# Window-attention block: values computed channel-major and turned by VectorE, instead of token-major by TensorE

## The chip, the cores and the metric

The kernel runs on one core of one Trainium2 chip, in one launch. The metric is the device time of that launch in microseconds (us); the runs of the kernel before gave a median of 2942.57 us (2941.42 to 2943.20, three runs).

## The reference

The input x is [16, 192, 56, 56] in float32. The block is one layer of a shifted-window transformer; cut to what matters:

```
xl  = layernorm(x over its 192 channels) * norm1_w + norm1_b     # per pixel
xl  = roll(xl, (-3, -3));  windows of 7x7 = 49 tokens, 64 windows per image
q, k, v = xl @ qkv_w.T + qkv_b          # 6 heads of 32 channels each
attn = softmax(q @ k.T / sqrt(32))      # [49, 49] per window and head
out  = (attn @ v) @ proj_w.T + proj_b;  windows back to pixels, roll back
xl  = layernorm(out) * norm2_w + norm2_b
h   = gelu(xl @ fc1_w.T + fc1_b) @ fc2_w.T + fc2_b        # 768 hidden
return h + x
```

## The kernel before, in words

**Units and rounds.** The 56 x 56 picture is cut into 8 rows of windows. One row of windows (8 windows, T = 392 tokens) of one image is a *unit*; there are 128. The work on a unit is spread over many *rounds*: in each round every engine does one piece for several different units, in an order written out by hand in its own `step` function. `units(t)` gives the units: `u[k]` is unit t - k. The engines' own step numbers differ: round t on VectorE (DVE) and SyncE (SP) runs beside step t - 1 on GpSimd (POOL) and beside step t - 3 on TensorE (PE). Nothing but semaphores ties the engines; each runs its list strictly in order and stops at a wait.

**Precision.** Weights and activations are split into a high and a low part (`x_h`, `x_l`), and the last 64 of 192 channels hold high and low stacked in one 128-partition tile (`x_r`). So one product takes five matmuls: `five` (L317 to L324, weights stationary, 392 tokens moving, channels out) or `five_tokens` (L326 to L334, 98 tokens stationary, 192 channels moving, tokens out).

**Queries, keys, values.** `qkv` makes three tiles by `five`. `values(u, j)` (L614) makes the values token-major, one pair of windows (98 tokens) at a time: four calls in a step, twenty matmuls. `v_out` (L1061) on DVE copies each of the two PSUM banks `vt` to the tile `vs` [98 tokens, pairs, channels]. `spread` (L438) on SP then issues four DMAs from `vs` into `vbd`, in which the values of two heads stand as a block-diagonal matrix. Each takes 49 partitions, 12 runs of 128 bytes on each. `weighted` (L586) on PE reads `vbd`.

**SP's list in round t** (L451 to L468): `load_groups(t)` (xg, for the statistics of the first norm), `stats_in(t-2)` (one DMA, `bc`), `spread(t-4)`, `stats_out(t-1)` (four DMAs, waits for POOL's `rstd(0)`), `store(t-7)` (waits for DVE's `finish_main` and POOL's `residual`), and `load` (x itself, `xt`) for the unit in the slot just stored.

**POOL's list in one of its steps** (L1251 to L1275): `scaled_probs(u[4],3)`, `hidden_lo_last(u[6])`, `scaled_probs(u[3],0)`, `rstd(0,u[0])`, `less_mean_rest(u[1])`, `times_rstd_rest(u[1])`, `rstd(1,u[4])`, `scaled_probs(u[3],1)`, `residual(u[6])`, `scaled_probs(u[3],2)`. `rstd(1)` gives the reciprocal deviation of the second norm, which DVE's `normalise` (L985) waits for. `residual` (L1246) writes the last 64 output channels, which `store` waits for.

**PSUM.** Eight banks are handed round in the order of `BANK_USES` (L61); `claim` (L486) on PE waits until the last reader of the bank's previous use is done. The values' two banks are claimed as `("vt", 0)` and `("vt", 1)`; before `("vt", 1)` the bank held `("x2", 1)`, last read by DVE's `x2_rest_lo` (L991).

The functions that the change touches:

Of the kernel before, what the change touches and what calls it, by code (L numbers as in the profile page):

```python
# [22 lines left out]
F32 = mybir.dt.float32  # L23
F32R = mybir.dt.float32r
# [10 lines left out]
T = NW * N  # L35
# [53 lines left out]
QKV_READS = {4: 6, 3: 8, 2: 10}  # L89
QK_COPIES = 10  # L90

VMOVES = 16 * 4


def nth(unit, per_unit, i):

    return unit * per_unit + (i + 1)


def swin_block_program(nc, x, n1w, n1b, qkv_wt, qkv_b, proj_wt, proj_b, n2w, n2b,  # L100
                       fc1_wt, fc1_b, fc2_wt, fc2_b, out):
    ctx = ExitStack()
    with ctx:
        def sb(name, shape, dt=F32):
            return ctx.enter_context(nc.sbuf_tensor(name, shape, dt))

        def sem(name):
            return ctx.enter_context(nc.semaphore(name))
# [7 lines left out]
        wq = [sb(f"wq_{p}", [128, NQ], F32R) for p in ("mh", "ml", "rh", "rl")]  # L116
        wp = [sb(f"wp_{p}", [128, CR + C], F32R) for p in ("mh", "ml", "rh", "rl")]
        w1 = [sb(f"w1_{p}", [128, NF], F32R) for p in ("mh", "ml", "rh", "rl")]
        w2h = sb("w2h", [128, MT, C], F32R)
        w2l = sb("w2l", [128, MT, CM], F32R)  # L120
        w2r = sb("w2r", [128, MT, 128], F32R)
# [46 lines left out]
        half_k = sb("half_k", [128, 2])  # L168
        bk = sb("bk", [128, 2])

        vbd = sb("vbd", [128, 2, 2, PAIRS, 3, WP])
        vs = sb("vs", [TP, 2, PAIRS, C])
        pr = sb("pr", [TP, PAIRS, HEADS * WP])
        mx = sb("mx", [TP, PAIRS, HEADS])
        sm = sb("sm", [TP, PAIRS, HEADS])
# [20 lines left out]
        def bank(name, i):  # L196

            return psum[:, BANK_OF[name, i], :]
# [30 lines left out]
        s_hi = {n: sem(f"hi_{n}") for n in ("x1", "x2", "o")}  # L229
        s_lo = {n: sem(f"lo_{n}") for n in ("x1", "x2", "o")}  # L230
        s_qkv = sem("qkv_in_sbuf")
        s_vs = sem("values_in_sbuf")
        s_vbd = [sem(f"vbd_ready_{i}") for i in range(2)]
        s_mx = sem("row_max")
        s_sub = sem("max_subtracted")
# [55 lines left out]
        def last_read(name, i, v):  # L291

            if name in ("x2", "o"):
                return s_lo[name], v, 3, 2 * i
            if name == "ln2":
                return s_norm, v, PAIRS, 2 * i + 1
            if name == "vt":
                return s_vs, v, 2, i
            if name == "qkv":
                return s_qkv, v, QK_COPIES, QKV_READS[i] - 1  # L300
            if name == "fc1":
                return s_gelu, v, MT, i
            if name == "fc2":
                return (s_ym, s_yr)[i], v, 1, 0
            return {"s": s_sub, "pt": s_ptc}[name], v, PAIRS, i
# [69 lines left out]
        def _(sp):  # L375
# [59 lines left out]
            sp.dma_start(b2[:, 0:1], fc2_b[0:CM].rearrange("(p a) -> p a", a=1)).then_inc(s_rest, 16)  # L435
            sp.dma_start(b2[0:CR, 1:2], fc2_b[CM:C].rearrange("(p a) -> p a", a=1)).then_inc(s_rest, 16)

            def spread(u):  # L438

                sp.wait_ge(s_vs, nth(u, 2, 1))  # L440
                if u > 1:

                    sp.wait_ge(s_pe["o"], nth(u - 2, 1, 0))
                src = vs[:, u % 2].rearrange("p j (a e d) -> p (j a) e d", a=3, e=2)
                dst = vbd[:, u % 2].rearrange("p i j a d -> p i (j a) d")
                for wi in range(2):
                    for e in range(2):
                        sp.dma_start(dst[WP * e:WP * e + N, wi, :, DH * e:DH * e + DH],
                                     src[N * wi:N * wi + N, :, e, :]).then_inc(s_vbd[u % 2], 16)

            for t in range(UNITS + 7):  # L451
                if t < UNITS:
                    if t > 2:
                        load_groups(t)
                    if 1 < t < AHEAD:
                        load(0, t)
                if 0 <= t - 2 < UNITS:
                    if t - 2 > 0:
                        stats_in(t - 2)
                if 0 <= t - 4 < UNITS:  # L460
                    spread(t - 4)
                if 0 <= t - 1 < UNITS:
                    if t - 1 > 0:
                        stats_out(t - 1)
                if 0 <= t - 7 < UNITS:
                    store((t - 7) // UPB, (t - 7) % UPB)
                    if t - 7 + AHEAD < UNITS:
                        load((t - 7 + AHEAD) // UPB, (t - 7 + AHEAD) % UPB)  # L468
# [14 lines left out]
        def _(pe):  # L483
# [102 lines left out]
            def weighted(u, j):  # L586
                if j == 0:
                    pe.wait_ge(s_vbd[u % 2], nth(u // 2, VMOVES, VMOVES - 1))
                    claim(u, [("o", 0), ("o", 1)], (s_ptc, PAIRS, 0))
                else:  # L590
                    claim(u, [], (s_ptc, PAIRS, j))


                for wi, p in ((0, 0), (0, 1), (1, 0), (1, 1), (0, 2), (1, 2)):
                    if p < 2:
                        w = 2 * j + wi
                        ps = bank("o", 0)[WP * p:WP * p + WP, N * w:N * w + N]
                    else:
                        ps = bank("o", 1)[WP * wi:WP * wi + WP, N * j:N * j + N]

                    block, side = (wi, p) if p < 2 else (2, wi)
                    last = nc.tensor.matmul(ps, vbd[0:KP, u % 2, wi, j, p, :], pt[:, j, block, N * side:N * side + N],  # L602
                                            start=True, stop=True)
                if j == PAIRS - 1:
                    last.then_inc(s_pe["o"], 1)
# [5 lines left out]
                if u == 0 and tile == 4:  # L611
                    hidden_bias_products()

            def values(u, j):  # L614
                c, cc = j // 2, j % 2
                if cc == 0:
                    claim(u, [("vt", c)], (s_lo["x1"], 2, 1))
                pairs = [p[:, TP * j:TP * j + TP] for p in x1]
                last = five_tokens(bank("vt", c)[0:TP, cc * C:(cc + 1) * C], wq, pairs)
                if cc == 1:  # L620
                    last.then_inc(s_pe["vt"], 1)

            def step(t, k, it):
                u = units(t)
                if u[0] is not None:
                    values(u[0], 0)
                if u[4] is not None:
                    fc2_lo(u[4], 3)
                if u[0] is not None:
# [2 lines left out]
                    fc2_lo(u[4], 4)  # L632
                    fc2_lo(u[4], 5)
                if u[0] is not None:
                    values(u[0], 1)
                    values(u[0], 2)
                if u[3] is not None:
                    fc1(u[3], 0)
                if u[0] is not None:
                    values(u[0], 3)  # L640
                if u[3] is not None:
                    fc1(u[3], 1)
                if u[0] is not None:
# [237 lines left out]
        def _(dve):  # L881
# [9 lines left out]
            def split(n, w, raw, cols, nw, scaled):  # L891

                sm_, sr_ = raw
                dve.wait_ge(s_raw[n], 16 * (18, 6, 3)[n])
                if nw is not None:
                    if n:
                        dve.wait_ge(s_split, n)
                    nc.vector.tensor_scalar(scl_m[:, 0:cols], sm_[:, 0:cols], nwb[:, nw:nw + 1], None, ALU.mult).then_inc(s_scaled, 1)
                    nc.vector.tensor_scalar(scl_r[:, 0:cols], sr_[:, 0:cols], nwb[:, nw + 1:nw + 2], None, ALU.mult).then_inc(s_scaled, 1)
                    scaled += 2  # L900
                    dve.wait_ge(s_scaled, scaled)
                    sm_, sr_ = scl_m, scl_r
                nc.vector.tensor_copy(w[0][:, :], sm_[:, 0:cols]).then_inc(s_scaled, 1)
                nc.vector.tensor_copy(w[2][:, :], sr_[:, 0:cols]).then_inc(s_scaled, 1)
                scaled += 2
                dve.wait_ge(s_scaled, scaled)
                nc.vector.tensor_tensor(w[1][:, :], sm_[:, 0:cols], w[0][:, :].bitcast(F32), ALU.subtract)

                low = CR if n == 1 else 128
                nc.vector.tensor_tensor(w[3][0:low, :], sr_[0:low, 0:cols], w[2][0:low, :].bitcast(F32), ALU.subtract).then_inc(s_split, 1)  # L910
                return scaled
# [149 lines left out]
            def v_out(u, c):  # L1061
                if u > 1:

                    dve.wait_ge(s_vbd[u % 2], nth(u // 2 - 1, VMOVES, VMOVES - 1))
                dve.wait_ge(s_pe["vt"], nth(u, 2, c))
                nc.vector.tensor_copy(vs[:, u % 2, 2 * c:2 * c + 2, :], bank("vt", c)[0:TP, 0:2 * C].rearrange("p (j n) -> p j n", j=2)).then_inc(s_vs, 1)

            def step(t, k, it):
                u = units(t)
# [133 lines left out]
        def _(pool):  # L1203
# [26 lines left out]
            def times_rstd_rest(u):  # L1230
                pool.wait_ge(s_yr1_sub, nth(u, 1, 0))
                nc.gpsimd.tensor_tensor(yr1[:, :], yr1[:, :], bc[0:CR, u % 2, :, 1], ALU.mult).then_inc(s_yr1, 1)

            def hidden_lo_last(u):
# [2 lines left out]
                b = (MT - 1) % HB  # L1237
                nc.gpsimd.tensor_tensor(hl[:, b, :], hf[:, b, :], hh[:, b, :].bitcast(F32), ALU.subtract).then_inc(s_hl_last, 1)  # L1238

            def scaled_probs(u, j):  # L1240

                pool.wait_ge(s_rec, nth(u, PAIRS, j))
                each = rc[:, j, :].unsqueeze(2).to_broadcast([TP, HEADS, N])
                nc.gpsimd.tensor_tensor(probs(j), probs(j), each, ALU.mult).then_inc(s_prob, 1)  # L1244
# [6 lines left out]
            def step(t, k, it):  # L1251
# [10 lines left out]
                if u[1] is not None:  # L1262
                    if u[1] > 0:
                        less_mean_rest(u[1], (k - 1) % SLOTS)
                    if u[1] > 0:
                        times_rstd_rest(u[1])
                if u[4] is not None:
                    rstd(1, u[4])
                if u[3] is not None:
# [35 lines left out]
```

## Time and profile before

| | |
|---|---|
| median of three runs | 2942.57 us |
| profiled execution: span from first to last instruction | 2938.0 us |
| PE busy | 2892.5 us (98%) |
| DVE busy | 2630.3 us (90%) |
| ACT (ScalarE) busy | 2686.3 us (91%) |
| POOL busy | 1364.7 us (46%) |
| SP queue waiting for POOL's residual, in total | 947.0 us, 128 times |

The page gives no other time for the profiled execution than its span; the median of the runs is 4.6 us above it. Matmuls are pipelined, so the duration of one is longer than the distance to the next start; for what a matmul costs, starts are to be compared. An SP row in a timeline is the time that the queue needs to issue a DMA, not the transfer; "us to landing" counts from there to the last byte.

### The profile page before, as it was taken

What the parts mean: (1) busy time and instruction counts of PE and PEld (TensorE: products, weight loads), DVE (VectorE), ACT (ScalarE), POOL (GpSimd) and SP (SyncE); (2) the same over time, 40 slices, a digit from 0 to 9 for tenths busy, and PEclk for the clock granted to TensorE, in tenths of its full rate; (3) what the DMA queues carried; (4) which work ended last, traced back from release to release, by engine and by line L of the source; (5) the groups of instructions that cost most, each with busy time, mean ns of one, the idle gap of its engine ahead of it and who ended that gap; (6) DMA issues with size and microseconds to landing.
All of it is one profiled execution on the core that took longest, in us unless ns stands there. A gap on an engine that the chain in (4) does not pass through costs nothing.

```text
span 2938.0 us, 74792 instructions
## 1 busy us (share of the span) xinstructions
PE 2892.5 (98%) x26284; PEld 2823.9 (96%) x26284; DVE 2630.3 (90%) x7211; ACT 2686.3 (91%) x5500; POOL 1364.7 (46%) x1549
## 2 busy tenths in 40 slices
PE   5999999999999999999999999999999999999998
PEld 5999999999999999999999999999999999999998
DVE  7899999998999999999999999998999999999985
ACT  3899999999999999999999999999999999999996
POOL 3444444444444444444544444444445444444442
PEclk9999999999999999999999999999999999999999
DMA  5333333323333333333333333333333333333321
GB/s 111 58 77 76 69 73 76 74 68 78 77 69 72 74 78 68 76 78 70 70 73 81 68 72 78 73 68 77 79 68 72 76 77 67 76 74 74 69 62 26
DMA packets 645586, 213.10 MB, mean 73 GB/s; under 512 B 500835, under 2 KB 628580, under 8 KB 645220
## 3 DMA queue, kind: packets, MB, share of 16 engines
q1 hardware_dynamic: 641284, 206.65, 32.3%
q8 instruction: 217, 3.56, 0.6%
q10 hardware_dynamic: 3936, 1.68, 0.3%
q14 instruction: 149, 1.22, 0.2%
HBM read 130.69 MB, written 38.94 MB: 58 GB/s over the span
## 4 chain that ended last, share of the span: by engine, by line
PE 97%; DVE 1%; SPq 1%; ACT 0%; issue 0%; DMA 0%; POOL 0%; POOLq 0%; DVEq 0%; ACTq 0%
PE psum L320 8%; PE psum L321 7%; PE psum L322 7%; PE psum L324 7%; PE psum L323 7%; PE psum L602 7%; PE psum L576 6%; PE psum L556 5%; PE psum L567 5%; PE psum L557 5%; PE psum L568 5%; PE psum L558 5%; PE psum L582 4%; PE psum L330 4%; PE psum L332 3%; PE psum L331 3%
## 5 line engine op out<-in xcount | busy, mean ns | idle before, releaser
L1244 POOL TENSOR_TENSOR pr<-pr,rc 98x294 f32<-98x294 f32 x512 | 385.6, 763 | 378.8 <-DVE rc L1059 378.8
L758 ACT ACTIVATE hh<-psum,b 128x392 fp32r<-128x392 f32 x768 | 451.3, 588 | 47.7 <-PE psum L568 39.0
L761 ACT ACTIVATE hf<-psum,b 128x392 f32<-128x392 f32 x768 | 450.9, 587 | 6.3
L1217 POOL TENSOR_TENSOR ve<-mv,eps 104x4 f32<-104x4 f32 (+1 forms) x256 | 80.6, 315 | 753.5 <-DVE mv L983 753.5
L1238 POOL TENSOR_TENSOR hl<-hf,hh 128x392 fp32r<-128x392 f32 x128 | 226.0, 1766 | 374.4 <-ACT hf L761 374.4
L1046 DVE TENSOR_REDUCE mx<-psum 98x6 f32<-98x294 f32 x512 | 232.5, 454 | 133.3 <-PE psum L577 129.3
L1023 DVE TENSOR_TENSOR hl<-hf,hh 128x392 fp32r<-128x392 f32 x640 | 347.7, 559 | 3.7 <-ACT hf L761 3.7
L320 PE MATMUL psum<-x_h,w_mh 128*128 128x392 f32 x768 | 274.9, 358 | 0.7 <-DVE pr L1051 0.6
L556 PE MATMUL psum<-hh,w2h 128*128 128x392 f32 x768 | 272.9, 355 | 0.0
L715 ACT ACTIVATE pt<-psum 113x294 f32<-113x294 f32 x512 | 206.1, 403 | 70.7 <-PE psum L582 70.4
L576 PE MATMUL psum<-km,qm 128*98 128x98 f32 x2048 | 261.7, 250 | 7.3 <-DVE xn L988 3.4
L567 PE MATMUL psum<-hl,w2h 128*128 128x392 f32 x768 | 264.7, 345 | 0.3 <-POOL hl L1238 0.3
L557 PE MATMUL psum<-hh,w2l 128*128 128x392 f32 x768 | 262.0, 341 | 0.0
L321 PE MATMUL psum<-x_h,w_ml 128*128 128x392 f32 x768 | 261.6, 341 | 0.0
L322 PE MATMUL psum<-x_l,w_mh 128*128 128x392 f32 x768 | 261.2, 340 | 0.0
L568 PE MATMUL psum<-hl,w2h 128*64 128x392 f32 x768 | 260.6, 339 | 0.0
L324 PE MATMUL psum<-x_r,w_rl 128*128 128x392 f32 x768 | 260.5, 339 | 0.0
L323 PE MATMUL psum<-x_r,w_rh 128*128 128x392 f32 x768 | 260.4, 339 | 0.0
L558 PE MATMUL psum<-hh,w2r 128*128 128x392 f32 x768 | 259.5, 338 | 0.0
L975 DVE BATCH_NORM_STATS2 st<-psum 98x6 f32<-98x192 f32 x512 | 184.2, 360 | 73.3 <-PE psum L334 68.6
L576 PEld LDWEIGHTS psum<-km,qm 128*98 128x98 f32 x2048 | 237.7, 167 | 11.4 <-issue 6.5
L1051 DVE TENSOR_TENSOR pr<-psum,mx 98x294 f32<-98x294 f32 x512 | 234.2, 457 | 4.2
(144 smaller groups left out, 10396.6 us busy)
## 6 DMA issues: line engine op xcount, KB each, us to landing
bc<-mean_rstd SPq DMA_DIRECT2D x128, 392.0 KB, 3.6
vbd<-vs SPq DMA_DIRECT2D x512, 73.5 KB
xg<-in_x SPq DMA_DIRECT2D x368, 96.0 KB, 2.5
xt<-in_x SPq DMA_DIRECT2D x112, 194.5 KB, 2.7
out<-xt SPq DMA_DIRECT2D x112, 194.5 KB, 1.9
xt<-in_x SPq DMA_DIRECT2D x112, 97.2 KB, 2.5
out<-xt SPq DMA_DIRECT2D x112, 97.2 KB, 2.1
mean_rstd<-mv SPq DMA_DIRECT2D x384, 1.0 KB
```

The costliest lines, as they stand in the source:

```text
L320: nc.tensor.matmul(ps, wmh[:, c0:c0 + m], xh, start=True, stop=False)
L321: nc.tensor.matmul(ps, wml[:, c0:c0 + m], xh, start=False, stop=False)
L322: nc.tensor.matmul(ps, wmh[:, c0:c0 + m], xl, start=False, stop=False)
L323: nc.tensor.matmul(ps, wrh[:, c0:c0 + m], xrr, start=False, stop=False)
L324: return nc.tensor.matmul(ps, wrl[:, c0:c0 + m], xrr, start=False, stop=True)
L556: nc.tensor.matmul(ym, w2h[:, m, 0:CM], hh[:, b, :], start=a, stop=False)
L557: nc.tensor.matmul(ym, w2l[:, m, :], hh[:, b, :], start=False, stop=False)
L567: nc.tensor.matmul(ym, w2h[:, m, 0:CM], hl[:, b, :], start=False, stop=z)
L568: nc.tensor.matmul(yx[0:CR], w2h[:, m, CM:C], hl[:, b, :], start=False, stop=z, skip_group_check=True).then_inc(s_pe["fc2"], 1)
L576: nc.tensor.matmul(ps[:, TP * wi:TP * wi + TP], qm[:, w, :], km[:, w, :], start=True, stop=True)
L758: nc.scalar.activation(hh[:, m % HB, :], bank("fc1", m)[:, 0:T], ACT.Gelu, bias=b1[:, m:m + 1]).then_inc(s_hh, 1)
L761: nc.scalar.activation(hf[:, m % HB, :], bank("fc1", m)[:, 0:T], ACT.Gelu, bias=b1[:, m:m + 1]).then_inc(s_gelu, 1)
```

## The change

- **PE.** The twenty matmuls of `values` become eight with 392 moving columns. `values_main` makes the first 128 value channels by `five`. `values_rest` makes the last 64 with three matmuls, against the new weights `wv_m` and `wv_r`, whose columns 0 to 63 are the high and 64 to 127 the low part of the weight; the result is two summands, on partitions 0 to 63 and 64 to 127. `values_rest` stands at the head of PE's step, `values_main` where `values(1)` and `values(2)` stood, and `values(3)` is gone.
- **DVE.** The copies in `v_out` become two `transpose` instructions that read the PSUM bank as 8 windows x 2 blocks x 32 tokens and turn each 32 x 32 block. The second block of a window starts at its token 17, so 15 tokens come twice. Results: `vt_m` (main) and `vt_r` (rest).
- **SP and POOL.** `low_part(u)` (one DMA, 64 partitions of 2048 bytes) brings partitions 64 to 127 of `vt_r` to `vt_l`; POOL's new `last_values(u)` adds it to partitions 0 to 63. It stands in front of `rstd(1)` in POOL's step, and `low_part` behind the spreads in SP's round.
- **Spreads.** Twelve DMAs in place of four: for each of six heads one of 32 partitions and one of 17, each with 8 runs of 128 bytes.
- Four small DVE operations at the start split `wv_m` and `wv_r`.

```diff
-VMOVES = 16 * 4
+VMOVES = 16 * 12
...
+            def low_part(u):
+                sp.wait_ge(s_vt, nth(u, 2, 0))
+                if u > 0:
+                    sp.wait_ge(s_vsum, nth(u - 1, 1, 0))
+                sp.dma_start(vt_l[:, :, :, :], vt_r[CR:128, u % 2]).then_inc(s_vlow, 16)
+
+            def spread(u, head, src):
+                p, e = head // 2, head % 2
+                r = DH * head if head < 4 else DH * (head - 4)
+                dst = vbd[:, u % 2, :, p, DH * e:DH * e + DH]
+                sp.dma_start(dst[WP * e:WP * e + DH], src[r:r + DH, u % 2, :, 0, :]).then_inc(s_vbd[u % 2], 16)
+                sp.dma_start(dst[WP * e + DH:WP * e + N], src[r + 2 * DH - N:r + DH, u % 2, :, 1, :]).then_inc(s_vbd[u % 2], 16)
+
+            def spread_main(u):
+                sp.wait_ge(s_vt, nth(u, 2, 1))
+                if u > 1:
+                    sp.wait_ge(s_pe["o"], nth(u - 2, 1, 0))
-                src = vs[:, u % 2].rearrange("p j (a e d) -> p (j a) e d", a=3, e=2)
-                dst = vbd[:, u % 2].rearrange("p i j a d -> p i (j a) d")
-                for wi in range(2):
-                    for e in range(2):
-                        sp.dma_start(dst[WP * e:WP * e + N, wi, :, DH * e:DH * e + DH],
-                                     src[N * wi:N * wi + N, :, e, :]).then_inc(s_vbd[u % 2], 16)
+                for head in range(4):
+                    spread(u, head, vt_m)
+
+            def spread_rest(u):
+                sp.wait_ge(s_vsum, nth(u, 1, 0))
+                for head in range(4, HEADS):
+                    spread(u, head, vt_r)
...
                 if 0 <= t - 4 < UNITS:
-                    spread(t - 4)
+                    spread_main(t - 4)
+                    spread_rest(t - 4)
+                if 0 <= t - 3 < UNITS:
+                    low_part(t - 3)
...
+            def values_main(u):
+                claim(u, [("vt", 1)])
+                five(bank("vt", 1)[:, 0:T], wq, 0, CM, [p[:, :] for p in x1]).then_inc(s_pe["vt"], 1)
+
+            def values_rest(u):
+                claim(u, [("vt", 0)], (s_lo["x1"], 2, 0))
+                ps = bank("vt", 0)[:, 0:T]
+                nc.tensor.matmul(ps, wv_m[:, :], x1[0][:, :], start=True, stop=False)
+                nc.tensor.matmul(ps, wv_m[:, :], x1[1][:, :], start=False, stop=False)
+                pe.wait_ge(s_lo["x1"], nth(u, 2, 1))
+                nc.tensor.matmul(ps, wv_r[:, :], x1[2][:, :], start=False, stop=True).then_inc(s_pe["vt"], 1)
...
-                nc.vector.tensor_copy(vs[:, u % 2, 2 * c:2 * c + 2, :], bank("vt", c)[0:TP, 0:2 * C].rearrange("p (j n) -> p j n", j=2)).then_inc(s_vs, 1)
+                blocks = bass.AP(psum, BANK_OF["vt", c] * 512, [[8 * 512, 128], [N, NW], [N - DH, 2], [1, DH]])
+                nc.vector.transpose((vt_r, vt_m)[c][:, u % 2], blocks).then_inc(s_vt, 1)
...
+            def last_values(u):
+                pool.wait_ge(s_vlow, 16 * (u + 1))
+                nc.gpsimd.tensor_tensor(vt_r[0:CR, u % 2], vt_r[0:CR, u % 2], vt_l[:, :, :, :], ALU.add).then_inc(s_vsum, 1)
...
                     if u[1] > 0:
                         times_rstd_rest(u[1])
+                if u[2] is not None:
+                    last_values(u[2])
                 if u[4] is not None:
                     rstd(1, u[4])
```

## Rows read from the trace of the kernel before

**Rows 1.** The page: busy time of each engine and the granted clock.

```profile
PE 2892.5 (98%) x26284; PEld 2823.9 (96%) x26284; DVE 2630.3 (90%) x7211; ACT 2686.3 (91%) x5500; POOL 1364.7 (46%) x1549
PEclk9999999999999999999999999999999999999999
```

**Rows 2.** Busy time by window (us, busy and count per engine), one round.

```profile
1000.00:1022.40 22.40, 22.40 (x208) 21.91 (x206) 20.35 (x57) 21.00 (x44) 10.62 (x12) 1.00 0.35 75
```

**Rows 3.** Waits in total: who waited for whom, us, times, longest.

```profile
DVE mx L1046 <- PE psum L577: 129.3, 126, 2.2
SPq L412 <- POOL xt L1249: 947.0, 128, 16.1
```

**Rows 4.** Timeline of PE (start, duration), parts of one step.

```profile
1005.08 0.34 PE L320 MATMUL psum<-x_h,wq_mh 128*128 128x392 f32 x1
...
1005.97 0.34 PE L567 MATMUL psum<-hl,w2h 128*128 128x392 f32 x1
...
1006.67 0.25 PE L330 MATMUL psum<-wq_mh,x_h 128*98 128x192 f32 x1
...
1007.57 0.38 PE L320 MATMUL psum<-x_h,w_mh 128*128 128x392 f32 x1
```

**Rows 5.** Groups of DVE: the copy that goes, a transpose that stays.

```profile
L1066 DVE COPY vs<-psum 98x384 f32<-98x384 f32 x256 | 138.6, 542 | 5.8 <-PE psum L334 1.9
L954 DVE STREAM_TRANSPOSE xtok<-xg 128x768 f32<-128x768 f32 x128 | 123.9, 968 | 0.1
```

**Rows 6.** Timeline of SP: issues from a store to the spreads, one round.

```profile
1019.22 0.36 SPq L414 DMA_DIRECT2D out<-xt  x1
...
1028.49 0.41 SPq L407 DMA_DIRECT2D bc<-mean_rstd  x1
1029.00 3.65 SPq L448 DMA_DIRECT2D vbd<-vs  x4
```

**Rows 7.** The same of a later round: first store, xg, first spread.

```profile
1064.05 0.36 SPq L414 DMA_DIRECT2D out<-xt  x1
...
1069.08 2.52 SPq L390 DMA_DIRECT2D xg<-in_x  x5
...
1072.18 0.89 SPq L448 DMA_DIRECT2D vbd<-vs  x1
```

**Rows 8.** Timeline of POOL from the second norm's rstd on.

```profile
1015.80 0.43 POOL L1217 TENSOR_TENSOR ve<-mv,eps 98x4 f32<-98x4 f32 x1 [3.74 <-DVE mv L983]
...
1018.13 1.01 POOL L1249 TENSOR_TENSOR xt<-yr,xt 64x392 f32<-64x392 f32 x1
```

**Rows 9.** DMA issues: count, KB each, median us to landing.

```profile
bc<-mean_rstd SPq DMA_DIRECT2D x128, 392.0 KB, 3.6
vbd<-vs SPq DMA_DIRECT2D x512, 73.5 KB
xt<-in_x SPq DMA_DIRECT2D x112, 97.2 KB, 2.5
mean_rstd<-mv SPq DMA_DIRECT2D x384, 1.0 KB
```

**Rows 10.** Two half-microseconds while the spreads move; last columns DMA share, GB/s.

```profile
1032.50:1033.00 0.50, 0.50 (x5) 0.50 (x3) 0.50 (x2) 0.47 (x2) 0.50 (x1) 1.00 0.60 94
1033.00:1033.50 0.50, 0.50 (x6) 0.48 (x5) 0.50 (x1) 0.50 (x2) 0.42 (x2) 1.00 0.60 94
```

**Rows 11.** Timeline of DVE: the last read of the bank `("x2", 1)`; normalise.

```profile
1005.93 0.75 DVE L994 TENSOR_TENSOR x_r<-psum,x_r 64x196 fp32r<-64x196 f32 x2
...
1017.67 0.85 DVE L988 TENSOR_SCALAR xn<-psum,mv,rs 98x192 f32<-98x192 f32 x2
```

More of the change, by code:

```diff
@@ L118, in swin_block_program @@
         w1 = [sb(f"w1_{p}", [128, NF], F32R) for p in ("mh", "ml", "rh", "rl")]
+        wv_m = sb("wv_m", [128, 128], F32R)
+        wv_r = sb("wv_r", [128, 128], F32R)
         w2h = sb("w2h", [128, MT, C], F32R)
@@ L169, in swin_block_program @@
         bk = sb("bk", [128, 2])
-        vbd = sb("vbd", [128, 2, 2, PAIRS, 3, WP])
-        vs = sb("vs", [TP, 2, PAIRS, C])
+        vbd = sb("vbd", [128, 2, NW, 3, WP])
+        vt_m = sb("vt_m", [128, 2, NW, 2, DH])
+        vt_r = sb("vt_r", [128, 2, NW, 2, DH])
+        vt_l = sb("vt_l", [CR, NW, 2, DH])
         pr = sb("pr", [TP, PAIRS, HEADS * WP])
@@ L231, in swin_block_program @@
         s_qkv = sem("qkv_in_sbuf")
-        s_vs = sem("values_in_sbuf")
+        s_vt = sem("values_by_token")
+        s_vlow = sem("low_part_of_last_values_moved")
+        s_vsum = sem("last_values_summed")
         s_vbd = [sem(f"vbd_ready_{i}") for i in range(2)]
@@ L297, in last_read @@
             if name == "vt":
-                return s_vs, v, 2, i
+                return s_vt, v, 2, i
             if name == "qkv":
@@ L436, in _ @@
             sp.dma_start(b2[0:CR, 1:2], fc2_b[CM:C].rearrange("(p a) -> p a", a=1)).then_inc(s_rest, 16)
-            def spread(u):
-                sp.wait_ge(s_vs, nth(u, 2, 1))
+            def low_part(u):
[11 more added lines that the diff above has]
+                sp.wait_ge(s_vt, nth(u, 2, 1))
                 if u > 1:
                     sp.wait_ge(s_pe["o"], nth(u - 2, 1, 0))
-                src = vs[:, u % 2].rearrange("p j (a e d) -> p (j a) e d", a=3, e=2)
-                dst = vbd[:, u % 2].rearrange("p i j a d -> p i (j a) d")
-                for wi in range(2):
-                    for e in range(2):
-                        sp.dma_start(dst[WP * e:WP * e + N, wi, :, DH * e:DH * e + DH],
-                                     src[N * wi:N * wi + N, :, e, :]).then_inc(s_vbd[u % 2], 16)
+                for head in range(4):
[4 more added lines that the diff above has]
+                    spread(u, head, vt_r)
             for t in range(UNITS + 7):
@@ L601, in weighted @@
                     block, side = (wi, p) if p < 2 else (2, wi)
-                    last = nc.tensor.matmul(ps, vbd[0:KP, u % 2, wi, j, p, :], pt[:, j, block, N * side:N * side + N],
+                    last = nc.tensor.matmul(ps, vbd[0:KP, u % 2, 2 * j + wi, p, :], pt[:, j, block, N * side:N * side + N],
                                             start=True, stop=True)
@@ L612, in qkv @@
                     hidden_bias_products()
[L614 to L621, printed above, removed]
+            def values_main(u):
[8 more added lines that the diff above has]
+                nc.tensor.matmul(ps, wv_r[:, :], x1[2][:, :], start=False, stop=True).then_inc(s_pe["vt"], 1)
             def step(t, k, it):
@@ L625, in step @@
                 if u[0] is not None:
-                    values(u[0], 0)
+                    values_rest(u[0])
                 if u[4] is not None:
@@ L634, in step @@
                 if u[0] is not None:
-                    values(u[0], 1)
-                    values(u[0], 2)
+                    values_main(u[0])
                 if u[3] is not None:
                     fc1(u[3], 0)
-                if u[0] is not None:
-                    values(u[0], 3)
                 if u[3] is not None:
@@ L907, in split @@
                 nc.vector.tensor_tensor(w[1][:, :], sm_[:, 0:cols], w[0][:, :].bitcast(F32), ALU.subtract)
+                if n == 0:
+                    for pair, raw_, of in ((wv_m, sm_, w[0]), (wv_r, sr_, w[2])):
+                        nc.vector.tensor_copy(pair[:, 0:CR], of[:, CM:C].bitcast(F32))
+                        nc.vector.tensor_tensor(pair[:, CR:128], raw_[:, CM:C], of[:, CM:C].bitcast(F32), ALU.subtract)
                 low = CR if n == 1 else 128
```

## The prediction, made before the changed kernel ran

> **What bounds the kernel now.** I read the busy times first: PE is busy for 98% of the span at a full clock [rows 1], and in a round from the middle for all 22.40 us, while DVE works 20.35, ACT 21.00 and POOL 10.62 us of it [rows 2]. The round repeats every 22.41 us: the stores of two rounds on start at 1019.22 and 1064.05 [rows 6, 7]. The totals of waits agree: DVE's largest is for PE (129.3 us), and SP stands 947.0 us, or 7.4 us a round, before its store, waiting for POOL's residual [rows 3]. So PE sets the time, the others follow it with 1.4 to 2 us to spare, and POOL and SP look idle. That idleness is a sum, though. Whether it helps depends on whether a closed chain through the two comes out shorter than PE's round, and the change closes such a chain.
>
> **PE.** Ten matmuls of `values` take 1006.67 to 1007.57, 0.090 us each; five with 392 columns take 1005.08 to 1005.97, 0.178 each [rows 4]. Removed: 20 x 0.090 = 1.80. Added: 8 x 0.178 = 1.42. PE's round becomes 22.41 - 0.38 = 22.03 us. `values_main` asks for its bank somewhat earlier than `values(2)` did: `values_rest` is 3 x 0.178 = 0.53 against 0.45 for `values(0)`, so it stands at 1006.75, and DVE's last read of that bank ends at 1006.68 [rows 11]. That fits by 0.07 us; any lateness of DVE there is now PE's. The four splits of the new weights at the start are small: less than two copies of 542 ns, say 1 us in all.
>
> **DVE.** No row has a 32 x 32 transpose out of PSUM. The nearest is the one of 768 elements in SBUF, 968 ns [rows 5]; by elements, 512 would be 645 ns. Ends: the copy that goes, 542 ns, and the full 968 ns. I take 645, so 2 x 0.10 = 0.2 us a round more (0 to 0.85), against 22.03 - 20.35 = 1.7 us of room.
>
> **SP and POOL: the new ring.** In round t, POOL's `last_values` waits for `low_part`, and behind it in POOL's list stand `rstd(1)`, `scaled_probs(1)` and `residual`. SP's `store` waits for that residual; behind the store stand the loads, `load_groups`, `stats_in`, the twelve spreads, and then the `low_part` of the next round, for which the next `last_values` waits. This is a closed chain, once round, with no other engine in it. Its length is a lower limit of the round. Before, the same queue order existed, but nothing led from the spreads back to POOL in the same round.
>
> Its fixed terms:
> - residual ends at 1018.13 + 1.01 = 1019.14, the store is issued at 1019.22 [rows 6, 8]: 0.08;
> - SP from the store to the first spread: 9.78 us [rows 6] in the two units of eight that have an extra pair of runs, 8.13 us [rows 7] in the other kind, six in eight: mean 8.5;
> - the sum in `last_values`, 64 x 512: by elements from the residual's 1.01 us for 64 x 392, 1.32, and 0.1 for the two semaphores: 1.42 (a row of 128 partitions would not be nearer);
> - from the start of `rstd(1)` to the end of the residual, 1015.80 to 1019.14 [rows 8]: 3.34.
> Sum 13.34 us. What is left is L, from the issue of the first spread to the landing of `low_part`.
>
> **L, from below.** If the twelve spreads only cost their issue, the nearest row is the xg transfer of 32 partitions with six runs each, five in 2.52 us, 0.50 each [rows 7]: 6.05 us. `low_part` (64 rows, 128 KB) is nearest to the xt of 64 rows and 97 KB, 2.5 us to landing [rows 9]. L = 8.55, ring 21.9 us, just under PE's 22.03.
>
> **L, with the packets.** While the old spreads move, the DMA engines carry 94 GB/s in runs of 128 bytes, that is 734 runs per us, flat over both stretches, at a share of 0.60 of 16 engines [rows 10]: 16 x 0.60 / 734 = 13.1 ns of recorded time for a run. A spread of 49 partitions can be dealt evenly only to 7 engines, and 734 / 7 = 105 per us is 9.5 ns for a run on one engine, if records overlap. Seventeen partitions cannot be dealt evenly to any number of engines up to 16 except one. A sign in the profile that dealing goes by whole partitions: the list of issues gives a time to landing for transfers of 128, 64 and 32 partitions, and leaves it out for the spreads (49) and for mean_rstd, which shares its semaphore with a transfer of 8 partitions [rows 9]; their completions do not come in the usual count.
> If so, each 17-partition spread puts all its 136 runs on one engine, and each 32-partition one another 16: 6 x 152 = 912 runs in one line, 8.7 us at 9.5 ns, 11.9 us at 13.1 ns. The share of `low_part` on that engine stands behind them. The line starts late, because the 392 KB of `bc`, issued 0.5 us ahead and landing after 3.6 [rows 6, 9], is in front: some 2 us after the first spread is issued. With 1 us for the runs of `low_part` and its completion, L = 2 + 8.7 + 1 = 11.7, up to 14.9. I take 12.0, near the first, to which seven engines in the flat stretch point. Ring: 13.34 + 12.0 = 25.3 us a round.
>
> The Trainium skill says this of the dealing (DMA: Bandwidth & Descriptors, section "Why a DMA increments its semaphore by 16 and not by 1"): a transfer issued from SP uses the largest number of engines up to 16 that divides the slowest dimension on both sides. By it 49 gives 7, 17 gives 1; the missing landing times agree, and no row of before shows a transfer of 17. The same page (section "Anatomy of one DMA — SWDGE (gpsimd) path", its table of the fixed cost) speaks the other way: many descriptors can be emitted before their added cost shows. By that alone the lower L would hold, and the first rival below.
>
> **The sum.** The ring exists when a store and a `low_part` share the rounds, about 124 of them. 25.3 - 22.41 = 2.9 us, times 124 = 360. Span 2938.0 + 360 + 1 = 3299, and the runs stand 4.6 above the profiled span: 3303 us. PE's gain of 0.38 is not lost on top of this, it merely turns into waiting. What is late then: POOL's `rstd(1)`, which ended just before DVE's `normalise` at 1017.67 [rows 8, 11]. A spread started at 1006.65 would have `low_part` landed at 1018.7 and `rstd(1)` done at 1021.8, so DVE, and PE behind it at the transposes of `xn` and of the probabilities, stand for it.
>
> **Rivals.**
> 1. *The short ring* (0.13). The 17-row spreads flow as freely as the rest: for it speak the flat rate and the low share of the DMA engines (0.35 in a round [rows 2]); against it the missing landing times. Ring 21.9 to 22.9 by L = 8.55 to 9.5, with PE's floor at 22.03: span 2938 - 0.38 x 124 + 1 = 2892 at the floor, so 2896, up to 2938 + 0.5 x 124 = 3000. Mostly faster.
> 2. *SP itself is held* (0.04). If issuing a 17-row spread lasts as long as its runs at 13.1 ns, 1.8 us, the twelve take 6 x 1.8 + 6 x 0.55 = 14.1 us, `low_part` lands 2.5 later and the ring is 13.34 + 16.6 = 29.9 us: about 3870 us. The old spreads took 3.65 us for four [rows 6], no longer than their runs, which speaks for it in part.
> 3. *DVE takes over* (0.03). The transposes at 968 ns and more, plus PE's wait at the `("vt", 1)` bank, bring DVE's 20.35 to 21.2; only with twice that price would it pass 22.4 and end near the time of before, 2943.
>
> The one with the other sign is the first; it decides from L below 9.0 us (22.41 - 13.34).
>
> **Chances and range.** The long ring has 0.80. Its own range follows from L = 10 to 14: 23.3 to 27.3 us a round, 3050 to 3550 us. I give 3000 to 3500: below lies most of rival 1, above rival 2 and the top of L, together about 0.2. A difference under 0.2% (6 us) is what a measurement here cannot tell from none. Faster: 0.09 from rival 1 and a little from 3, 0.10. Same: 0.04. Slower: 0.86.
>
> **What would show it.** Right: SP's stores start 25 us apart; POOL has a wait before `last_values` named after the DMA into `vt_l`, some 6 us a round; `vt_l` lands several us after its issue, against 2.5 for xt; DVE's `normalise` waits for `rs`, PE for `pr` or `xn`; PE is busy some 87% of the span; SP's wait for the residual shrinks only moderately. Wrong: `vt_l` lands within 2.7 us and rounds of 22.0 to 22.4 us (rival 1); no idle SP before the store (2); DVE busy over 95% (3). The number falls with L alone: each us in L is 124 us.

## The result: 3369.8 us, slower by 14.5%

| | before | changed |
|---|---|---|
| median | 2942.65 us | 3369.81 us (3363.77 to 3374.49, four runs) |
| ratio, 95% interval | | 1.145 (1.144 to 1.146) |
| profiled span | 2938.0 us | 3369.7 us |
| PE / DVE / ACT / POOL busy | 98 / 90 / 91 / 46% | 90 / 81 / 80 / 41% |
| SP idle before its store | 947.0 us | 558.0 us |

The forecast was 3303 us, with 3000 to 3500. One of the four executions of run 2 below took 3113.6 us, at a granted clock of 0.849 against 0.995 and more in the other three, and its ratio is taken from those three. The page of the changed kernel, in the lines that answer to [rows 1] and the two lines of the chain that ended last:

```profile
PE 3033.3 (90%) x24748; PEld 2875.4 (85%) x24748; DVE 2715.9 (81%) x7215; ACT 2699.3 (80%) x5500; POOL 1386.2 (41%) x1677
...
PEclk8999999999999999999999999999999999999999
...
SPq 62%; POOL 15%; DMA 10%; issue 6%; PE 4%; DVE 2%; ACT 0%; POOLq 0%; DVEq 0%; ACTq 0%
SPq L460 19%; SPq L461 15%; SPq L399 10%; DMA vt_l<-vt_r 10%; SPq L390 5%; POOL vt_r L1284 5%; SPq L424 4%; SPq L391 4%; POOL rs L1262 4%; SPq L423 4%; POOL xt L1295 3%; POOL pr L1290 2%; SPq L416 2%; POOL ve L1258 1%; PE psum L605 0%
```

The chain no longer runs through PE, which had 97% of it before and has 4% now. It is SP's queue for 62%, POOL for 15% and the landing of `vt_l` for 10%. L460 and L461 are the spreads of 32 and of 17 partitions, L453 is `low_part`, L1284 the sum in `last_values`. The totals of waits (who waited for whom, us, times, longest) say the same from the other side:

```profile
POOL vt_r L1284 <- DMA vt_l<-vt_r: 869.3, 126, 8.7
DVE xn L1025 <- POOL rs L1262: 459.1, 123, 6.3
...
ACT pt L747 <- PE psum L611: 361.3, 169, 7.2
...
PE psum L605 <- DVE xn L1025: 235.5, 116, 6.7
...
SPq L421 <- POOL xt L1295: 558.0, 128, 13.2
```

POOL stands 6.9 us in each of 126 rounds for the low part; behind it DVE stands for `rs`, PE for `xn`, ACT for PE. One link of the ring in the timeline of SP, for [rows 6]:

```profile
1105.07 0.37 SPq L416 DMA_DIRECT2D bc<-mean_rstd  x1
1105.55 0.68 SPq L460 DMA_DIRECT2D vbd<-vt_m  x1
1106.27 0.73 SPq L461 DMA_DIRECT2D vbd<-vt_m  x1
1107.05 0.95 SPq L460 DMA_DIRECT2D vbd<-vt_m  x1
1108.05 0.66 SPq L461 DMA_DIRECT2D vbd<-vt_m  x1
...
1114.68 0.66 SPq L461 DMA_DIRECT2D vbd<-vt_r  x1
1115.45 0.84 SPq L453 DMA_DIRECT2D vt_l<-vt_r  x1
1116.39 1.69 SPq L408 DMA_DIRECT2D mean_rstd<-mv  x3
1118.12 0.33 SPq L409 DMA_DIRECT2D mean_rstd<-mv  x1
1122.48 0.36 SPq L423 DMA_DIRECT2D out<-xt  x1
...
1131.04 0.68 SPq L460 DMA_DIRECT2D vbd<-vt_m  x1
```

and in that of POOL, for [rows 8]:

```profile
1109.90 1.05 POOL L1273 TENSOR_TENSOR yr<-yr,bc 64x392 f32<-64x392 f32 x1
1118.26 1.28 POOL L1284 TENSOR_TENSOR vt_r<-vt_r,vt_l 64x512 f32<-64x512 f32 x1 [7.32 <-DMA vt_l<-vt_r]
1119.50 0.19 POOL L1258 TENSOR_TENSOR ve<-mv,eps 98x4 f32<-98x4 f32 x1
1119.77 1.01 POOL L1262 TENSOR_TENSOR rs<-ve,half 98x4 f32<-98x4 f32 x1
1120.76 0.68 POOL L1290 TENSOR_TENSOR pr<-pr,rc 98x294 f32<-98x294 f32 x1
1121.40 1.01 POOL L1295 TENSOR_TENSOR xt<-yr,xt 64x392 f32<-64x392 f32 x1
```

First spread 1105.55, `low_part` issued 1115.45 (9.90 later), POOL's sum from 1118.26 (2.81) to 1119.54 (1.28), residual done 1122.41 (2.87), store 1122.48 (0.07); the next first spread follows at 1131.04 (8.56). That is 25.5 us. Over 113 rounds of the trace the mean terms are 9.95, 2.84, 1.28, 2.87, 0.07 and 8.86, together 25.9 us, and the stores stand 25.9 us apart. PE, which before was never idle in a round [rows 2], now has 3.2 us without work in one stretch of 26 us and runs at a lower granted clock in the next (0.87, the third number from the end); a round has some 3.9 us over the 22.0 that its list was put at:

```profile
1096.00:1122.00 26.00, 22.84 (x195) 21.56 (x196) 21.18 (x59) 21.07 (x43) 10.96 (x15) 1.00 0.31 68
1122.00:1148.00 26.00, 25.66 (x196) 24.61 (x196) 21.78 (x57) 21.26 (x43) 11.58 (x14) 0.87 0.30 69
```

### The profile page after: what moved, and what is told of

Its sections match the earlier page's. It is cut to its first block, busy times and chain, and to the rows that moved or that the text cites. A ratio compares the mean times of both kernels' runs of the same rounds, so it can differ in the third digit from the quotient of the medians.

```text
span 3369.7 us, 73004 instructions
## 1 busy us (share of the span) xinstructions
PE 3033.3 (90%) x24748; PEld 2875.4 (85%) x24748; DVE 2715.9 (81%) x7215; ACT 2699.3 (80%) x5500; POOL 1386.2 (41%) x1677
## 4 chain that ended last, share of the span: by engine, by line
SPq 62%; POOL 15%; DMA 10%; issue 6%; PE 4%; DVE 2%; ACT 0%; POOLq 0%; DVEq 0%; ACTq 0%
SPq L460 19%; SPq L461 15%; SPq L399 10%; DMA vt_l<-vt_r 10%; SPq L390 5%; POOL vt_r L1284 5%; SPq L424 4%; SPq L391 4%; POOL rs L1262 4%; SPq L423 4%; POOL xt L1295 3%; POOL pr L1290 2%; SPq L416 2%; POOL ve L1258 1%; PE psum L605 0%
## 5 line engine op out<-in xcount | busy, mean ns | idle before, releaser
L1025 DVE TENSOR_SCALAR xn<-psum,mv,rs 98x192 f32<-98x192 f32 x512 | 218.5, 469 | 459.2 <-POOL rs L1262 459.1
L1284 POOL TENSOR_TENSOR vt_r<-vt_r,vt_l 64x512 f32<-64x512 f32 x128 | 165.1, 1290 | 869.3 <-DMA vt_l<-vt_r 869.3
L1290 POOL TENSOR_TENSOR pr<-pr,rc 98x294 f32<-98x294 f32 x512 | 345.3, 684 | 418.8 <-DVE rc L1096 418.8
L605 PE MATMUL psum<-km,qm 128*98 128x98 f32 x2048 | 298.0, 273 | 240.9 <-DVE xn L1025 235.5
L605 PEld LDWEIGHTS psum<-km,qm 128*98 128x98 f32 x2048 | 259.4, 187 | 280.1 <-issue 276.0
L1279 POOL TENSOR_TENSOR hl<-hf,hh 128x392 fp32r<-128x392 f32 x128 | 179.4, 1401 | 306.2 <-ACT hf L793 306.2
L585 PE MATMUL psum<-hh,w2h 128*128 128x392 f32 x768 | 294.8, 384 | 0.0
L586 PE MATMUL psum<-hh,w2l 128*128 128x392 f32 x768 | 277.0, 361 | 0.0
L587 PE MATMUL psum<-hh,w2r 128*128 128x392 f32 x768 | 273.1, 356 | 0.0
L611 PE MATMUL psum<-ident,pr 98*128 98x98 f32 x1536 | 236.6, 269 | 35.2 <-POOL pr L1290 34.7
L330 PE MATMUL psum<-x_h,w_ml 128*128 128x392 f32 x768 | 261.7, 341 | 0.0
```

The source lines that it names most:

```text
L585: nc.tensor.matmul(ym, w2h[:, m, 0:CM], hh[:, b, :], start=a, stop=False)
L586: nc.tensor.matmul(ym, w2l[:, m, :], hh[:, b, :], start=False, stop=False)
L587: nc.tensor.matmul(yx, w2r[:, m, :], hh[:, b, :], start=a, stop=z, skip_group_check=True)
L605: nc.tensor.matmul(ps[:, TP * wi:TP * wi + TP], qm[:, w, :], km[:, w, :], start=True, stop=True)
L1284: nc.gpsimd.tensor_tensor(vt_r[0:CR, u % 2], vt_r[0:CR, u % 2], vt_l[:, :, :, :], ALU.add).then_inc(s_vsum, 1)
```

## Experiments

In all of them "round" is the distance between two starts of ACT's `o_h`, averaged over sixty rounds from the middle: 22.41 us before, 25.88 us in the changed kernel. Runs 2 and 8 were executed four times, the others once; the kernel before, executed beside them in two sets of seven, stayed between 2938.9 and 2942.3 us.

**1. Sixteen rows in place of 17.**

```diff
-                sp.dma_start(dst[WP * e + DH:WP * e + N], src[r + 2 * DH - N:r + DH, u % 2, :, 1, :]).then_inc(s_vbd[u % 2], 16)
+                sp.dma_start(dst[WP * e + DH:WP * e + N - 1], src[r + 2 * DH - N:r + DH - 1, u % 2, :, 1, :]).then_inc(s_vbd[u % 2], 16)
```

> The changed kernel with one row fewer in every second spread: 16 partitions in place of 17, so the value of token 48 of each window is left out; everything else, the twelve transfers and their 128-byte runs included, stays. Theory A (17 rows are dealt to one DMA engine, and SP's issue is held by the line on that engine): 16 rows go to 16 engines, a pair of spreads costs what the xg transfers cost, 2 x 0.5 us instead of 1.65, the way from the first spread to the landed low part shrinks from 12.7 to about 9 us, the ring from 25.6 to 22 us, and the time is 2900 to 2960. Rival B (each 128-byte run costs the same wherever it goes, 1.65 us for a pair of 392 runs): 384 runs instead of 392 change nothing, 3330 to 3370.

Measured 3145.4 us, round 24.04. This is in neither window: one partition fewer is worth 224 us, so rival B is out, and theory A holds in kind and not in size. The issues by line (duration ns min/median/max, first and last start) and the time to landing, of the changed kernel:

```profile
L460 SPq DMA_DIRECT2D vbd<-vt_m x512: 618/911/1896, 54.9 to 3317.7; - x171
...
L461 SPq DMA_DIRECT2D vbd<-vt_m x512: 649/662/747, 55.7 to 3318.5; - x171
```

and of the kernel with 16 rows:

```profile
L460 SPq DMA_DIRECT2D vbd<-vt_m x512: 591/600/1742, 54.1 to 3091.4; - x171
...
L461 SPq DMA_DIRECT2D vbd<-vt_m x512: 591/611/1568, 54.9 to 3092.1; - x171
DMA to landing us min/median/max: 1.9/2.0/4.4
```

One partition fewer, and it is mostly the *other* spread, the one issued behind it, that falls from 911 to 600 ns. The list also gives a landing time again, which it did not beside the transfers of 17 partitions. The twelve issues take 8.24 us instead of 9.95, and the round loses 1.84 us, of which 1.71 are these and 0.13 the way from the issue of the low part to the sum. What stays is 0.65 to 0.7 us for each issue, where I had 0.50.

**2. The low part first.**

```diff
+                if 0 <= t - 3 < UNITS:
+                    low_part(t - 3)
                 if 0 <= t - 4 < UNITS:
                     spread_main(t - 4)
                     spread_rest(t - 4)
-                if 0 <= t - 3 < UNITS:
-                    low_part(t - 3)
```

> The changed kernel with low_part issued ahead of the twelve spreads in SP's round instead of behind them; nothing is left out. Ring theory: the spreads are no longer between the store and POOL's add, that chain falls from 25.6 to some 16 us, and what is left is SP's own list, 21.3 us a round by its idle time (558 us in 128 rounds of 25.6), and PE's 22.0: 22.0 to 22.6 us a round, 2890 to 2970. If instead SP's queue or the DMA engines are the bound, or POOL's added work as such: unchanged, 3330 to 3380.

Measured 2993.3 us, ratio to before 1.017 (1.015 to 1.019), round 22.80. Moving one DMA gives back 376 of the 427 us: the ring is the cause. It missed the expected window by 23 us; run 3 explains most of that. The queue is still in its chain (the page: DVE 38%, PE 26%, SPq 18%).

**3. No low part.**

```diff
-                if 0 <= t - 3 < UNITS:
-                    low_part(t - 3)
...
-                sp.wait_ge(s_vsum, nth(u, 1, 0))
...
-                if u[2] is not None:
-                    last_values(u[2])
```

> The changed kernel without low_part, without POOL's last_values and without the wait for it; the low half of the last 64 value channels' sum is left out, the twelve spreads stay as they are. Ring theory: nothing leads from the spreads back to POOL, so PE's list is the bound again, 22.0 us a round, 2890 to 2920; it also prices PE's gain, 0.38 to 0.45 us a round. If the twelve spreads on SP were the bound by themselves: above 3200.

Measured 2973.3 us, round 22.67: no ring, but 0.64 us over PE's expected 22.03, above the window by 53 us and above the kernel before. The expectation was wrong, and so was the floor in the prediction. PE waits, in the totals and in its timeline (last column: idle before and for whom):

```profile
PE psum L339 <- DVE vt_m L1104: 39.4, 123, 0.3
...
1204.64 0.34 PE L333 MATMUL psum<-x_r,wq_rl 128*128 128x392 f32 x1
1205.31 0.30 PE L339 MATMUL psum<-wp_mh,o_h 128*98 128x192 f32 x1 [0.32 <-DVE vt_m L1104]
...
1215.47 0.34 PE L603 MATMUL psum<-kr,qr 128*98 128x98 f32 x2
...
1227.97 0.30 PE L339 MATMUL psum<-wp_mh,o_h 128*98 128x192 f32 x1 [0.31 <-DVE vt_m L1104]
```

and DVE's timeline:

```profile
1203.53 0.88 DVE L1033 SCALAR_TENSOR_TENSOR o_r<-psum,bq,o_r 64x196 fp32r<-64x196 f32 x2
1204.44 0.72 DVE L1104 STREAM_TRANSPOSE vt_m<-psum 128x512 f32<-128x512 f32 x1
...
1215.85 0.47 DVE L1080 TENSOR_REDUCE mx<-psum 98x6 f32<-98x294 f32 x1 [1.02 <-PE psum L603]
...
1217.74 0.57 DVE L1051 TENSOR_TENSOR x_l<-psum,x_h 128x392 fp32r<-128x392 f32 x1 [0.21 <-ACT x_h L744]
...
1227.11 0.72 DVE L1104 STREAM_TRANSPOSE vt_m<-psum 128x512 f32<-128x512 f32 x1
```

L339 is `project(0)`. It claims the bank `("ln2", 0)`, which is bank 6, the one that held `("vt", 1)`; DVE's second transpose must have read it. This is a second closed chain. PE from `project(0)` at 1205.31 to the scores that DVE waits for until 1215.85 is 10.54 us; DVE from that `row_max(0)` to the transpose's end at 1227.83 is 11.98 us; with 0.14 us from the transpose to the next `project(0)` it is 22.66 us, the distance of the two L339 rows. These are distances between events, so they add up to the round by themselves. Where the chain runs is said by the page, and it takes ACT in between PE and DVE: DVE stands a second time behind the scores, 0.21 us at 1217.74, for ACT's `x_h`, and that wait ends later.

```profile
PE 47%; DVE 37%; issue 7%; ACT 6%; SPq 2%; DMA 0%; POOL 0%; POOLq 0%; DVEq 0%; ACTq 0%
```

That the bank ties PE to DVE is tested in run 7. In the kernel before the same claim was met with little to spare. There `project(0)` (L330) starts 0.27 us after DVE's second copy ends, where the release alone takes 0.14 us (run 3), so the slack was 0.13 us:

```profile
1009.92 0.56 DVE L1066 COPY vs<-psum 98x384 f32<-98x384 f32 x1
...
1010.75 0.25 PE L330 MATMUL psum<-wp_mh,o_h 128*98 128x192 f32 x1
```

The second chain also explains run 2: with it as a floor, 22.67 us, only 0.13 us a round of that run stay unexplained, and no run isolates them.

**4. The kernel before, with twelve spreads.**

```diff
-VMOVES = 16 * 4
+VMOVES = 16 * 12
...
-                        sp.dma_start(dst[WP * e:WP * e + N, wi, :, DH * e:DH * e + DH],
-                                     src[N * wi:N * wi + N, :, e, :]).then_inc(s_vbd[u % 2], 16)
+                        for p in range(3):
+                            sp.dma_start(vbd[WP * e:WP * e + N, u % 2, wi, :, p, DH * e:DH * e + DH],
+                                         vs[N * wi:N * wi + N, u % 2, :, 2 * DH * p + DH * e:2 * DH * p + DH * e + DH]).then_inc(s_vbd[u % 2], 16)
```

> The kernel before with its four spreads cut into twelve (one for each pair of windows' side, head of a pair and pair of heads: 49 partitions with 4 runs each); same bytes, same runs, nothing left out. Ring theory: without a way from the spreads back to POOL the longer issue (0.5 to 0.9 us each, 6 to 11 us in place of 3.8) is hidden in SP's 7.4 idle us a round: 2940 to 2960. Rival (twelve transfers are too many for SP wherever they stand): 3100 or more.

Measured 2948.1 us, round 22.43. SP's idle time before its store falls from 947.0 to 167.9 us and the time moves by 0.2%, as the ring theory had it. Twelve transfers a round cost next to nothing as long as nobody waits behind them.

**5. The sum at the end of POOL's step.**

```diff
-                if u[2] is not None:
-                    last_values(u[2])
                 if u[4] is not None:
                     rstd(1, u[4])
...
                     scaled_probs(u[3], 2)
+                if u[2] is not None:
+                    last_values(u[2])
```

> The changed kernel with POOL's last_values moved from in front of rstd(1) to the end of POOL's step; nothing is left out. Ring theory: the residual, and so SP's store, no longer wait for the low part, the chain through store, spreads and add is open, and what is left is the second chain seen in the run without a low part: DVE from row_max(0) to the second transpose, 11.98 us, and PE from project(0), which claims that transpose's bank, to scores(0), 10.66 us: 22.67 us a round, 2970 to 2985. SP's own list, some 22.2 us a round with the low part, stands just under it. If POOL's add as such were the cost: unchanged at 3370.

Measured 2975.3 us, round 22.67, inside the window and as with the low part left out. The ring is opened at its other joint, every piece of work kept; so neither the transfer nor POOL's 1.28 us is a cost of its own here, and the second chain is what remains.

**6. Every spread of 32 partitions.**

```diff
-                sp.dma_start(dst[WP * e + DH:WP * e + N], src[r + 2 * DH - N:r + DH, u % 2, :, 1, :]).then_inc(s_vbd[u % 2], 16)
+                sp.dma_start(dst[WP * e + DH:WP * e + 2 * DH], src[r:r + DH, u % 2, :, 1, :]).then_inc(s_vbd[u % 2], 16)
...
-                blocks = bass.AP(psum, BANK_OF["vt", c] * 512, [[8 * 512, 128], [N, NW], [N - DH, 2], [1, DH]])
+                blocks = bass.AP(psum, BANK_OF["vt", c] * 512, [[8 * 512, 128], [N, NW], [DH, 2], [1, DH]])
```

(and the 16 PSUM columns behind token 391 are zeroed once)

> The changed kernel, order as it is, with the second block of each window at token 32 instead of 17, so that every spread has 32 partitions (rows 49 to 63 of vbd then hold other tokens' values, which meet zeros in pt); nothing is left out. Theory A (17 rows go to one engine, which holds the issue): as with 16 rows, 0.65 to 0.7 us for each of twelve issues, 8.1 us in place of 9.95, the ring 24.0, 3130 to 3160. Rival B (the runs count, 3072 now against 2352): 9.95 x 3072 / 2352 = 13.0 us, the ring 28.9, 3700 or more.

Measured 3155.5 us, inside theory A's window, round 24.10; the issues take 8.33 us, the median of one is 611 ns. That is 30% more runs of 128 bytes than in the changed kernel and 1.6 us less. The number of runs is not what SP pays for here; the count of partitions is.

**7. Sum last, main values turned first.** As 5, and:

```diff
-                    v_out(u[3], 0)
+                    v_out(u[3], 1)
                 if u[5] is not None:
                     o_rest_lo(u[5])
                 if u[3] is not None:
-                    v_out(u[3], 1)
+                    v_out(u[3], 0)
```

(the counts of `s_vt` follow the new order)

> As the one before last (last_values at the end of POOL's step), and DVE turns the main values first and the rest of the values behind o_rest_lo, so that the bank that project(0) claims is free a transpose earlier; nothing is left out. Second-chain theory: 22.67 - 0.7 = 21.97 us of that chain, and then SP's own list is the bound, 22.2 to 22.5 us: 2920 to 2955. If the bank is not what PE waits for: 2970 to 2985 as with last_values moved alone.

Measured 2916.8 us, 3 us below the window, round 22.18. The wait of L339 for `vt_m` is gone from PE's list (38.9 us in 5), and the round is 0.49 us shorter for the order of two instructions on DVE: just what PE loses there in run 3, where L339 starts 0.67 us after the matmul before it and 0.18 us is the usual step. The second chain is shown. The expectation that SP's list would be the next bound was wrong: the page gives PE 92% of the chain and SP's queue 4%.

**8. All three.**

> The changed kernel with all three: last_values at the end of POOL's step, the main values turned first, every spread of 32 partitions; nothing is left out. SP's list falls by some 1.8 us to 20.4, the second chain is 21.97, PE's list 22.0: 22.0 to 22.1 us a round, 2890 to 2905, 1.3 to 1.8% under the kernel before. If a fourth wait takes over: between 2905 and 2950.

Measured 2911.1 us, ratio to before 0.990 (0.989 to 0.992), round 22.13. This beats both kernels, by 1.0% and by 13.6%, and lies 6 us above the window of the first case. PE's list is the bound again, as the page's chain says:

```profile
PE 96%; SPq 1%; DVE 1%; ACT 0%; DMA 0%; issue 0%; POOL 0%; POOLq 0%; DVEq 0%; ACTq 0%
```

A small wait of PE's weight load is left:

```profile
PEld psum L329 <- DVE x_r L1033: 23.1, 124, 1.0
```

which is `values_main` waiting for `x2_rest_lo`, 0.19 us a round, the place where the prediction had counted 0.07 us of room.

## Why the prediction was right, and where not

**The ring: right.** It was named with its members, its order and its victims, and most of its signs are in the profile: stores 25.9 us apart, 6.9 us of DMA wait in front of `last_values`, `normalise` waiting for `rs`, PE for `xn` and `pr`. One sign failed: `vt_l` was to land several us after its issue and lands after 2.7, which had been listed among the signs of the short ring. The low part is late because it is issued late. Two cuts at different joints (2 and 5) and the removal of the transfer (3) each open it; twelve transfers without the way back do nothing (4).

| term, us a round | forecast | measured |
|---|---|---|
| residual to store | 0.08 | 0.07 |
| store to first spread | 8.5 | 8.86 |
| twelve spreads issued | in L | 9.95 |
| low part: issue to sum | in L | 2.84 |
| L together | 12.0 | 12.79 |
| sum | 1.42 | 1.28 |
| `rstd(1)` to residual | 3.34 | 2.87 |
| ring | 25.3 | 25.9 |

The measured ring gives 2938 + (25.88 - 22.41) x 124 = 3368 us against the 3369.7 of the profile. So the method of the sum holds. The 67 us between forecast and result are the 0.6 us by which the ring is longer (0.8 in L, 0.4 behind the store, and 0.6 less in the other terms), some 70 us, less the 4.6 us that the forecast set between span and run. That gap is not a constant: the profiled execution of the changed kernel took 3371.5 us over a span of 3369.7.

**L: right in size, its working half right.** The step that was mis-sized is the price of an issue. The lower bound took the xg transfers (0.50 us each) for it; where partitions deal evenly a spread costs 0.65 to 0.7 with its gaps (1, 6), which is 8.3 us for twelve and not 6.05. The 17 partitions then cost, as the prediction had it, but 1.6 to 1.7 us a round, not the 3.45 that it put on top. The two errors nearly cancelled, so that the 12.0 came out near the measured 12.79 is in part luck.

The line of runs on one engine shows in the trace, by its rate. Between the bursts of the 32-partition spreads the changed kernel moves 14 GB/s at a share of 0.09; run 6, over its spreads, 58 GB/s at 0.37 (last two numbers; the first row is the changed kernel's, the second run 6's):

```profile
1109.50:1110.00 0.50, 0.29 (x3) 0.32 (x4) 0.50 (x2) 0.50 (x2) 0.42 (x2) 1.00 0.09 14
...
1135.25:1139.00 3.75, 3.73 (x27) 3.43 (x26) 3.38 (x7) 3.65 (x7) 3.16 (x4) 1.00 0.37 58
```

A share of 0.09 of 16 engines is 1.4 engines' recorded time, and 14 GB/s in runs of 128 bytes are about 109 a microsecond; the prediction had 105 for one engine. No record names the engine. By the packet records, over 90 rounds, the runs of a round begin 1.8 us after the first spread is issued (forecast 2), last 10.0 us (forecast 8.7; for 0.9 of the 10.0 the line stands still), and `vt_l` lands 1.0 us after the last (forecast 1).

But `low_part` does not stand long behind that line: it lands 2.7 us after its issue, and 2.4 in run 1, where there is no such line. Of the 1.84 us that the 17th partition costs, 1.71 are in SP's issues. Why a transfer behind one of 17 partitions takes SP longer is not shown. A full line on one engine need not be the reason: in run 4 a transfer of 49 partitions and 196 runs held SP for 783 ns, where 32 partitions and 256 runs took 611 in run 6:

```profile
L449 SPq DMA_DIRECT2D vbd<-vs x1536: 762/783/1680, 55.5 to 2898.3; - x192
```

The dealing rule cited from the Trainium skill (DMA: Bandwidth & Descriptors, section "Why a DMA increments its semaphore by 16 and not by 1") agrees with these runs in its consequence: 16 and 32 partitions behave alike, 17 does not. The other statement taken from that page, that many descriptors can be emitted before the cost shows (section "Anatomy of one DMA — SWDGE (gpsimd) path"), is made there for transfers issued by GpSimd; on SP these runs fit it, as 128 runs and 256 runs issue in the same 0.61 us (1, 6).

**PE's floor: wrong.** The prediction said 22.03 us for PE once the ring is away, and that DVE had 1.7 us of room. The step that failed is "DVE", which compared sums per round and checked the claim of `("vt", 1)` but not the next claim of that same bank by `project(0)`, where the room was 0.13 us (run 3). PE comes there 0.38 us earlier, by the forecast's own count of matmuls, and DVE 0.3 us later: the transposes took 684 and 717 ns instead of the forecast 645, against 542 for the copies. So PE and DVE, with ACT between them and each with idle time, closed a chain of 22.67 us, longer than PE's list and longer than the round before. PE's own gain was also smaller: 22.41 - 22.13 = 0.28 us in the last run, of the 0.38 forecast; the 0.19 us wait is large enough for the missing 0.10, but no run removes it. In the changed kernel itself this chain does not set the time, since the first ring is longer.

**The rivals.** The short ring (0.13) is excluded by L, 12.8 us and not below 9.0. SP held altogether is excluded at its price, 14.1 us for the twelve: they take 9.95, and SP has 558.0 us of idle time. In kind it came nearer than its chance of 0.04 suggests, since it is SP's issues that the 17 partitions lengthen. DVE as the bound is wrong in the form given, an engine at its limit (81% busy). Its near relative, the chain of PE, ACT and DVE, costs some 30 us over the kernel before in run 3, and 58 us by the difference of runs 5 and 7.

## What to carry to other kernels

Before adding a wait between two queues that look idle, follow the lists of both once round and add up the closed chain: idle 54% and 7.4 us a round did not help, because the wait joined a long list on SP to a short one on POOL. Making a piece of such a chain faster shortened it by just that piece (1 and 6: 1.8 us a round); moving one instruction took it away (2, 5: over 3 us). And whoever makes the busiest engine faster should look at each PSUM bank that it claims: the reader that was just in time is now late.

## What the runs showed of the hardware

**Partitions of a transfer.** With 17 partitions in every second transfer, the median issue of the 32-partition transfer behind it is 911 ns, with 16 or 32 it is 600 to 611 ns. Twelve issues take 9.95, 8.24 and 8.33 us. The transfers of 17 themselves take 662 ns, and those of 49 in run 4 783 ns.

**The clock.** In the changed kernel PE is idle from about 1119.7 to 1121.8, and the granted clock is half from 1123 to 1126 at least. The stretches (us, busy and count of PE, PEld, DVE, ACT, POOL, then clock, DMA share, GB/s):

```profile
1121.00:1122.00 1.00, 0.17 (x2) 0.20 (x3) 1.00 (x4) 0.00 (x0) 1.00 (x2) 1.00 0.00 0
1122.00:1123.00 1.00, 0.81 (x9) 0.62 (x8) 1.00 (x4) 0.15 (x1) 1.00 (x2) 0.85 0.00 0
1123.00:1124.00 1.00, 0.89 (x6) 0.89 (x7) 1.00 (x1) 0.81 (x3) 0.70 (x2) 0.50 0.56 199
1124.00:1125.00 1.00, 1.00 (x9) 1.00 (x8) 1.00 (x4) 0.31 (x1) 0.00 (x0) 0.50 0.61 118
1125.00:1126.00 1.00, 1.00 (x6) 1.00 (x5) 0.71 (x2) 0.45 (x2) 0.00 (x0) 0.50 0.05 1
```

At 1.2 instead of 2.4 GHz a matmul of 392 columns starts every 0.33 us instead of 0.18. The mean granted clock of the run was 0.958. The terms of the ring, none of which is PE's, already make up the whole round, so it should have cost nothing here; no run tests that.

**POOL beside an idle DVE.** In `rstd(1)` the longer of two small operations (duration ns min/median/max) took 1.21 us before and 1.01 us in the changed kernel, where DVE stands still meanwhile:

```profile
L1221 POOL TENSOR_TENSOR rs<-ve,half x128: 1007/1211/1275, 76.9 to 2912.2; 98x4 f32<-98x4 f32 x128
...
L1262 POOL TENSOR_TENSOR rs<-ve,half x128: 1010/1012/1275, 88.5 to 3343.9; 98x4 f32<-98x4 f32 x128
```

The shorter one in front of it took 0.43 us in [rows 8] and 0.19 us in the round of the timeline above. Together they are 0.44 of the 0.47 us by which the ring's fifth term came out short. With the low part left out (run 3) DVE works there again and the median is 1.21 us again; the reason was not tested.
